# W2 in two pieces a half over four column groups, 128-row adapter fillers, and small loads first: a conditional low-rank block and a recurrence

## The reference

```python
# layer 0, with x: (4, 512, 256), ada_emb = cond: (4, 256)
c = layernorm(ada_emb) * ln_gamma + ln_beta
w = gelu(c @ W1 + bias1) @ W2 + bias2                  # W2: (256, 8192)
a1, b1, a2, b2 = [t.reshape(B, D, R) for t in jnp.split(w, 4, axis=-1)]
u = jnp.einsum('btd,bdr->btr', x, a2)
mid = gelu(jnp.einsum('btd,dl->btl', x, base_down) + jnp.einsum('btr,blr->btl', u, b2))
v = jnp.einsum('blr,btl->btr', b1, mid)
out = jnp.einsum('btl,kl->btk', mid, base_up) + jnp.einsum('bkr,btr->btk', a1, v)
x = x + (x + out)
# layer 1, with h0 = cond
xW = jnp.einsum('ntd,dh->nth', x, Wx) + b
h_t = tanh(xW_t + h_(t-1) @ Wh)                        # 512 steps, one after the other
x = x + hs
```

## Time and profile before

| | us |
|---|---|
| three timed runs | 555.97, 550.74, 555.61 |
| their median | 555.61 |
| the profiled execution | 551.53 |
| its span, first to last instruction | 549.7 |
| TensorE busy | 511.1 (93%) |
| DVE busy | 296.5 (54%) |
| ACT busy | 176.5 (32%) |
| POOL busy | 21.9 (4%) |

### The profile page before, as it was taken

How to read it: one execution, slowest core, us unless ns; L and a number is a source line. 1 busy time by engine, 2 the same in 40 slices (tenths; PEclk the granted TensorE clock), 3 DMA queues, 4 the chain that set the end, 5 groups by cost and what they waited for, 6 DMA issues and landing times.

```text
span 549.7 us, 32433 instructions
## 1 busy us (share of the span) xinstructions
PE 511.1 (93%) x14388; PEld 439.2 (80%) x14388; DVE 296.5 (54%) x2262; ACT 176.5 (32%) x1154; POOL 21.9 (4%) x34
## 2 busy tenths in 40 slices
PE   6988999999999999999998999899999989998995
PEld 4224777899999999999998888888888888888884
DVE  1154666555656555565555555555555555555553
ACT  2010222333333434333333333333333333333322
POOL 2850000000000000000000000000000000000000
PEclk7698999999999999999999999999999999999998
DMA  8950000000000000000000000000000000000000
GB/s 295 383 185 2 3 4 3 13 5 14 4 13 5 14 4 4 16 4 14 4 14 5 14 4 14 4 7 11 5 14 4 13 5 13 4 14 5 8 9 12
DMA packets 11346, 16.01 MB, mean 29 GB/s; under 512 B 1715, under 2 KB 7106, under 8 KB 11202
## 3 DMA queue, kind: packets, MB, share of 16 engines
q1 hardware_dynamic: 10352, 13.37, 7.4%
q10 hardware_dynamic: 854, 0.57, 0.4%
HBM read 11.85 MB, written 2.10 MB: 25 GB/s over the span
## 4 chain that ended last, share of the span: by engine, by line
PE 89%; ACT 5%; issue 2%; DVE 1%; DMA 1%; ACTq 0%; DVEq 0%
PE bank L833 65%; PE bank L762 7%; ACT w_sb L429 5%; PE bank L803 3%; PE bank L808 3%; PE bank L656 2%; PE bank L790 2%; PE bank L649 1%; DMA beta_sb<-in_L_cond_ln_beta 1%; PE bank L771 1%; PE bank L635 1%; PE bank L757 1%; PE bank L671 1%; PE bank L820 1%; PE bank L676 0%
## 5 line engine op out<-in xcount | busy, mean ns | idle before, releaser
L833 PE MATMUL bank<-w_sb,whp 128*128 128x52 bf16 x6132 | 243.0, 186 | 25.1 <-ACT w_sb L429 24.8
L591 DVE TENSOR_TENSOR r_ring<-w_sb 128x4 f32<-128x4 f32 x1022 | 136.5, 163 | 211.6 <-ACT w_sb L429 207.7
L429 ACT ACTIVATE w_sb<-bank 128x4 f32<-128x4 f32 x1024 | 142.0, 173 | 320.8 <-PE bank L833 320.8
L833 PEld LDWEIGHTS bank<-w_sb,whp 128*128 128x128 bf16 x6132 | 188.7, 96 | 68.4 <-ACT w_sb L429 46.4
L833 PE MATMUL bank<-r_ring,whp 128*128 128x52 bf16 x4096 | 219.9, 185 | 0.1
L833 PEld LDWEIGHTS bank<-r_ring,whp 128*128 128x128 bf16 x4096 | 173.9, 96 | 0.2 <-issue 0.2
L833 PE MATMUL bank<-l_ring,whp 128*128 128x52 bf16 (+1 forms) x2048 | 156.4, 177 | 0.0
L596 DVE TENSOR_TENSOR l_ring<-r_ring 128x4 bf16<-128x4 f32 x1024 | 136.3, 162 | 0.0
L833 PEld LDWEIGHTS bank<-l_ring,whp 128*128 128x128 bf16 x2048 | 121.6, 96 | 0.0
L762 PE MATMUL bank<-xp,wxp 128*128 128x32 bf16 x1536 | 71.6, 177 | 0.0
L762 PEld LDWEIGHTS bank<-xp,wxp 128*128 128x128 bf16 x1536 | 54.0, 96 | 0.0
(11 more groups left out here) (109 smaller groups left out, 192.3 us busy)
## 6 DMA issues: line engine op xcount, KB each, us to landing
w_sb<-in_L_cond_W SPq DMA_DIRECT2D x16, 512.0 KB, 10.8
x_sb<-in_x SPq DMA_DIRECT2D x4, 512.0 KB, 11.2
out<-o_sb SPq DMA_DIRECT2D x64, 32.0 KB, 1.6
down_sb<-in_L_cond_base_down SPq DMA_DIRECT2D x1, 256.0 KB, 5.2
w_sb<-in_L_cond_W ACTq DMA_DIRECT2D x1, 256.0 KB, 5.6
up_sb<-in_L_cond_base_up ACTq DMA_DIRECT2D x1, 256.0 KB, 9.0
wx_sb<-in_L_cond_Wx SPq DMA_DIRECT2D x1, 256.0 KB, 10.2
wh_sb<-in_L_cond_Wh SPq DMA_DIRECT2D x1, 256.0 KB, 10.4
```

Of the source, the lines that this page charges most:

```text
L429: nc.scalar.activation(h_ring[:, m, slot(pair, s), 0:B], zt, ACT.Tanh).then_inc(h_ready, 1)
L591: nc.vector.tensor_tensor(r_ring[:, k, q, 0:B], state_before(pair, s, k)[:, 0:B], state_hi_before(pair, s, k)[:, 0:B], ALU.subtract).then_ ...
L833: return nc.tensor.matmul(zbank(p, q, m)[:, col0:col0 + n], whp[part][:, k, P * m:P * (m + 1)], rhs[:, 0:n], start=False, stop=stop, skip_ ...
```

## The change

- **Loads.** W1 goes to SP, ahead of x. ACT issues cond, gamma, beta and bias1 first, and bias2 last, in four DMAs. Each half of W2 comes in four DMAs of 1 MB. ACT loads the table for Gelu right after the square root.
- **W2.** A half has two pieces of two chunks (1024 columns). `w_products` writes all four groups of 32 rows: even and odd chunk of each of the half's two types. There are 4 calls of 8 matmuls. `keep_rank` runs on 128 rows, 4 times. Copies on DVE and ACT bring the odd chunk's rows beside the even one's. The factors have a tile for each half.
- **Adapter products.** `a2m` and `b1m` are 128 rows high, zero outside 32 of them, so each product has 128 rows and is cut in two of 128 columns. ACT makes the masked copies. One list of 64 jobs (`job`), five a tile, two steps each, steps 0 to 9, now orders low-rank and unit products from tile 0, step 4, to tile 13.
- **Rest.** Both halves of v and a1 stand in the prologue. Input products have steps 10 to 15 but for 12: 11, 11, 11, 10 and 9 of them.

```diff
-        fac = sb("fac", [P, D])
+        fac = [sb(f"fac{h}", [P, NPC, 2, DC]) for h in range(2)]
...
-        facm = sb("facm", [P, B, D])
-        b1m = sb("b1m", [Q, B, D])
-        b2s = sb("b2s", [P, D])
+        a2m = sb("a2m", [P, B, D])
+        b1m = sb("b1m", [P, B, D])
...
-        SUMS, TURN, ROWS, PREFETCH = 3, 4, 5, 8
...
-        LOW, UNIT, ROWS_STEP = 1, 3, 12
+        SUMS, TURN, ROWS = 3, 4, 5
+
+
+
+
+
+
+        FILL, NJ, TURN_ROWS = 10, 5, 12
+        FIRST_J = 2
         NUNIT = B * (NTT - 1)
-        REST = {2: 2, 4: 5, 6: 6}
-
-        def unit_of(tile):
-            return 1 + (tile - UNIT) // B, (tile - UNIT) % B
-
-        def is_unit(tile):
-            return UNIT <= tile < UNIT + NUNIT
+        NMAKE = B * 8
+        NFILL = NMAKE + 4 * (NUNIT - B)
+        MOVE = (4, 5, 8, 9, 10)
+        REST = {2: 2, 4: 4, 6: 6}
+        INPUTS = (11, 11, 0, 11, 10, 9)
+        LOW_DOWN, LOW_UP, MID, UP = range(4)
+
+        def job(tile, j):
+            n = NJ * tile + j - FIRST_J
+            if not 0 <= n < NFILL:
+                return None
+            if n < NMAKE:
+                b, w = n // 8, n % 8
+                return (LOW_DOWN, LOW_UP, MID, UP)[w // 2], b, w % 2
+            return (MID, UP)[(n - NMAKE) % 4 // 2], B + (n - NMAKE) // 4, (n - NMAKE) % 2
...
+        def job_out(tile, j):
+            return bank[4 * (1 - tile % 2) + 1 + j % 3][:, P:P + D]
...
-                for c in range(NCH):
+                for c in range(NPC):
                     for k in range(K2):
-                        sp.dma_start(w2_sb[:, k, j:j + 2, CH * c:CH * (c + 1)],
-                                     w2v[k, :, j:j + 2, CH * c:CH * (c + 1)]).then_inc(ld_w2[h][c][k], 16)
-
+                        sp.dma_start(w2_sb[:, k, j:j + 2, 2 * CH * c:2 * CH * (c + 1)],
+                                     w2v[k, :, j:j + 2, 2 * CH * c:2 * CH * (c + 1)]).then_inc(ld_w2[h][c][k], 16)
+
+            sp.dma_start(w1_sb[:], W1.rearrange("(k p) n -> p k n", p=P)).then_inc(ld_w1, 16)
...
+            for h in range(2):
+                nc.gpsimd.memset(fac[h][:], 0.0).then_inc(zeroed, 1)
+            nc.gpsimd.memset(a2m[:], 0.0).then_inc(zeroed, 1)
+            nc.gpsimd.memset(b1m[:], 0.0).then_inc(zeroed, 1)
...
-            act.dma_start(bias2_sb[:], bias2.rearrange("(j n) -> j n", j=NTYPE)).then_inc(ld_bias2, 16)
-            act.dma_start(w1_sb[:], W1.rearrange("(k p) n -> p k n", p=P)).then_inc(ld_w1, 16)
...
+                for t in range(2):
+                    j = min(HALVES[h]) + t
+                    act.dma_start(bias2_sb[NTYPE * h + 2 * t:NTYPE * h + 2 * (t + 1)],
+                                  bias2.rearrange("(j c e n) -> j e c n", j=NTYPE, e=2, n=CH)[j]).then_inc(ld_bias2, 16)
...
+            nc.scalar.preload_act_table(ACT.Gelu)
...
+            act.wait_ge(fac_ready[0], NPC)
+            act.wait_ge(zeroed, 4)
+            nc.scalar.copy(fac[0][ROWS1, :, 1], fac[0][ODD1, :, 0]).then_inc(b2_ready, 1)
...
+            for b in range(B):
+                nc.scalar.mul(a2m[ROWS1, b], factor(0, ROWS0), bmask[ROWS0, b:b + 1]).then_inc(a2m_ready, 1)
...
-                rows = slice(Q * min(HALVES[h]), Q * min(HALVES[h]) + 2 * Q)
                 dve.wait_ge(w_ready[h], c + 1)
-                tmp = wmul[rows, c % 2].rearrange("p (d r) -> p d r", r=RANK)
+                tmp = wmul[:, c].rearrange("p (d r) -> p d r", r=RANK)
                 then_wait(nc.vector.tensor_tensor(
-                    tmp, bank[c][rows, :].rearrange("p (d r) -> p d r", r=RANK),
-                    rmask[rows].unsqueeze(1).broadcast_to([2 * Q, DC, RANK]), ALU.mult))
-                nc.vector.tensor_reduce(fac[rows, DC * c:DC * (c + 1)], tmp, AX.X, ALU.add).then_inc(fac_ready[h], 1)
+                    tmp, bank[NPC * h + c][:].rearrange("p (d r) -> p d r", r=RANK),
+                    rmask[:].unsqueeze(1).broadcast_to([P, DC, RANK]), ALU.mult))
+                nc.vector.tensor_reduce(fac[h][:, c, 0], tmp, AX.X, ALU.add).then_inc(fac_ready[h], 1)
...
+            for c in range(NPC):
                 keep_rank(0, c)
-            keep_rank(1, 0)
+            nc.vector.tensor_copy(fac[0][ROWS0, :, 1], fac[0][ODD0, :, 0]).then_inc(a2_ready, 1)
...
+            def move_low(tile, j, which, b, k):
+                dve.wait_ge(low_psum, 4 * b + 2 * (which - LOW_DOWN) + k + 1)
+                dst, base = (wd, down_sb) if which == LOW_DOWN else (wu, upT)
+                nc.vector.tensor_tensor(dst[:, b, k], job_out(tile, j), base[:, k], ALU.add).then_inc(low_moved, 1)
...
-                    for j in HALVES[h]:
-                        last = nc.tensor.matmul(bank[c][Q * j:Q * (j + 1), :],
+                    for g in range(NTYPE):
+                        j, e = HALVES[h][0] + g // 2, 2 * c + g % 2
+                        last = nc.tensor.matmul(bank[NPC * h + c][Q * g:Q * (g + 1), :],
...
+                    if i < FILL and (made := job(tile, i // 2)):
+                        if made[0] in (LOW_DOWN, LOW_UP):
+                            low_product(tile, i // 2, i % 2, *made)
+                        if made[0] == MID:
+                            mid_product(tile, i // 2, i % 2, made[1], made[2])
+                        if made[0] == UP:
+                            up_product(tile, i // 2, i % 2, made[1], made[2])
+                    if tile < NUNIT and i == TURN_ROWS:
                         turn_rows(tile)
-                    if i >= PREFETCH and not (last and p == 1):
-                        if i == PREFETCH:
+                    if i >= FILL and not (last and p == 1):
+                        if i == FILL:
 
                             pe.wait_ge(xp3_ready, tile + 2)
                             if p == 0 and not first:
                                 pe.wait_ge(o_ready, pair)
                             if tile == 0:
-                                pe.wait_ge(x2_rest, 4)
-                        e = i - PREFETCH
-                        if i < ROWS_STEP or i > ROWS_STEP + 1:
-                            input_products(1 - p, e // 4, e // 2 % 2, [e % 2])
-                        if i == ROWS_STEP + 1:
-                            input_products(1 - p, 1, 0, range(K2))
+                                pe.wait_ge(x2_rest, 6)
+                        e = i - FILL
...
+            def low_product(tile, j, e, which, b, k):
+                if which == LOW_DOWN:
+                    pe.wait_ge(a2m_ready, b + 1)
+                    left, right = a2m, fac[0]
                 else:
                     pe.wait_ge(b1m_ready, b + 1)
-                    left, right = b1m[:, b], fac[Q * A1:Q * (A1 + 1), :]
-                if i >= 3:
-                    pe.wait_ge(low_moved, B * K2 * which + i - 2)
-                nc.tensor.matmul(low_out(LOW + which, i), left[:, P * k:P * (k + 1)], right, start=True,
-                                 stop=True).then_inc(low_psum, 1)
-
-            def unit_product(tile, i):
-                t, b = unit_of(tile)
-                u, n, k = tile - UNIT, i // 2 % K2, i % K2
-                if i == 0:
+                    left, right = b1m, fac[1]
+                ins = nc.tensor.matmul(job_out(tile, j)[:, P * e:P * (e + 1)], left[:, b, P * k:P * (k + 1)],
+                                       right[:, e].rearrange("p e n -> p (e n)"), start=True, stop=True)
+                if e == 1:
+                    ins.then_inc(low_psum, 1)
```

More of the change, by code:

```diff
@@ L517, in make_x2 @@
                     in1=bank[4 + n][:].rearrange("p (b t) -> p b t", b=B)[:, :, t0:t1], op0=ALU.mult, op1=ALU.add)
-            mask_v(0)
+            for h in range(2):
+                mask_v(h)
             for n in range(K2):
@@ L675, in v_product @@
             def v_product(h, k):
-                last = nc.tensor.matmul(columns(bank[6][0:Q, B * HQ * h:B * HQ * (h + 1)]), b1T[:, k],
+                last = nc.tensor.matmul(columns(bank[6 + h][0:Q, 0:B * HQ]), b1T[:, k],
                                         mid0[:, k, :, HQ * h:HQ * (h + 1)], start=(k == 0), stop=(k == K2 - 1))
@@ new lines, in low_product, with mid_product @@
+                    left, right = b1m, fac[1]
[3 more added lines that the diff above has]
+                    ins.then_inc(low_psum, 1)
+            def mid_product(tile, j, k, u, m):
+                t, b = unit_of(u)
+                if k == 0 and m == 0:
+                    pe.wait_ge(rows_moved, u + 1)
+                    if u < B:
+                        pe.wait_ge(low_moved, 4 * b + 2)
+                    else:
+                        pe.wait_ge(x2_fill, K2 * (u - 1))
+                ins = nc.tensor.matmul(job_out(tile, j)[:, 0:P], wd[:, b, k, P * m:P * (m + 1)],
+                                       xT[:, k, b, P * t:P * (t + 1)], start=(k == 0), stop=(k == K2 - 1))
+                if k == K2 - 1:
+                    ins.then_inc(fmid_psum, 1)
@@ new lines, in up_product @@
+            def up_product(tile, j, k, u, n):
+                b = unit_of(u)[1]
```

(8 more changed lines are left out.)

226 lines of the change are left out of this document (101 added, 125 removed).

## The result

The changed kernel takes 547.9 us (median of 20 executions, 537.0 to 550.4), the kernel before 552.7 (median of 20, 550.7 to 557.3). The executions of the changed kernel lie in two groups, 6 at 537.0 to 542.0 and 14 at 546.5 to 550.4. The ratio of times, which compares the lower group with the executions of before, is 0.976, interval 0.973 to 0.980; the two medians alone have the ratio 0.991. The profiled execution took 548.2 us, its span 546.4, and belongs to the upper group.

What follows compares the result with a forecast made beforehand. TensorE was taken as the bound, a prologue to 53.2 us and then 512 steps. From the profiled 551.5 us, -3.3 -1.5 -3.2 -3.5 = -11.5 gave 540.0; for spread between runs it predicted 541.5, range 534 to 549.

Steps and rivals of the forecast that it cites:

- the sum: Whole kernel: prologue -3.3, tile 0 -1.5, tile 1 -3.2, tile 2 -3.5, together -11.5 us from 551.5, so 540.0.
- Fillers: Loop, tiles 1 and 2: products of 128 rows by 128 columns cost nothing, giving back 3.2 and 3.5 us.
- Rival 3: Loop, tiles 0 to 6: low-rank fillers not free, 6.7 us come back, 546.7 us; chance 0.10.
- Tile 0: Loop's first 16 steps: v and a1 products leave, 1.5 us less, bounds 0.7 and 2.2.
- Four column groups: Prologue, W2 products: four groups run side by side, 1.84 us a call, eight calls become four.
- rival 2: Prologue, W2 calls: column groups run in pairs only, 9.1 us more, 549.1 us; chance 0.08.
- factor of 1.3: Prologue, W2 calls: by a speedup of 3.07 a call takes 1.3 times as long, sum 2.7 us higher; not adopted.
- bias2: Prologue: its four DMAs, last on ACT's list, land at 11.0 us and hold all of TensorE's program behind.
- rival 1: Prologue: bias2 lands much later, 17.1 instead of 11, 6.1 us more, 546.1 us; chance 0.12.
- The small loads: Prologue loads: beta's 8.9 us wait goes, but W2 products start at 20.9 instead of 19.8, costing 1.1 us.
- Zeroing on POOL: Prologue: zeroing, ACT's copies and masks cost nothing beside TensorE; an uncovered mask or copy, a few tenths of a us.
- Rival 4: Prologue: granted clock stays at 0.5 past 24.4 up to the loop, slower than before, 562 us; chance 0.04.

Runs made afterwards that it cites:

- both: Changed kernel with the first bias product moved behind the base-down products and POOL's ring memset waiting for DVE's copy of the odd A2 rows; 537.4 us, ratio 0.970.
- bias_product_later: Changed kernel with the first bias product and its wait for the bias2 DMAs moved behind both base-down products; 538.2 us, ratio 0.976.
- memset_after_copy: Changed kernel with POOL's memset of the ring padding waiting until DVE's copy of the odd A2 rows is done; 543.2 us, ratio 0.984.
- changed_five_rounds: Changed kernel, unaltered, in six more executions, the first profiled; 538.6, 537.9, 541.2, 549.1, 541.6 and 549.2 us.
- copy_on_act: Changed kernel with the copy of the odd A2 rows moved from DVE to ACT, POOL's zeroing not made to wait; 540.1 us, ratio 0.976.
- low_rank_256_columns: Changed kernel with each low-rank filler whole, 128 rows by 256 columns, in one step of each pair and none in the other; 553.0 us.

## Why the prediction was right in the loop and wrong in the prologue

The prediction was 541.5 us, 534 to 549. The median, 547.9, lies 6.4 above it, near the upper bound, and the sign and the chance of "faster" were right. That the median is inside the range is luck: the upper part was there for rivals 1 to 3, none of which came, and what filled it was no rival. The lower group, 537 to 542, is the case that the sum describes; 14 of 20 executions are not in it.

**Fillers: right.** Tiles 1 and 2 gave back 3.2 and 3.45 (forecast 3.2 and 3.5). The rule "128 rows by 128 columns costs nothing" from the earlier trace rows carried over to zero-padded rows. Rival 3 falls, and the two experiments on fillers show that its price is real where rows are not filled up or columns not cut.

**Tile 0: right,** 15.45 (forecast 15.8). It still holds one step of 1.34 us whose surplus the chain calls issue; the experiments have 15.05 where that step is missing.

**Four column groups: right.** 16 instructions in 1.85 to 1.90, forecast 1.84; rival 2 falls. The three groups at once of the earlier trace rows were the row to go by. The Trainium skill, "TensorE: Matmul & The Clock Gate", Part 3, gives the speedup of 3.07 for four row tiles; for column tiles, which these are, it has only three (2.38), so the prediction's factor of 1.3 was carried over from another case. This trace has the full four: 16 instructions in four groups take 1.85 to 1.90, and the 4 of the u product, in one group, 1.89 at the high clock.

**bias2: right.** Landed at 10.98, forecast 11.0, so rival 1 (17.1) falls. The order of issue gave 8.9 to 11.7; that 11.0, picked between them, is hit within 0.02 is luck. The prediction also said that it would be late next and hold all of TensorE's program; this costs 3.4 us of W2's start in `both` and 6.9 in bias_product_later. The small loads brought nothing for that reason.

**The step that failed: "Zeroing on POOL, the copies and adapter masks on ACT ... lie beside TensorE's work and are costed at nothing".** The prediction priced DVE's small copy at nothing and POOL's zeroing at nothing, each by itself, and did not ask whether the two meet. What it gave as a bound for an uncovered copy, "a few tenths of a us", was taken from DVE alone and was 4.5. It never laid the new chain's times beside POOL's list, where a single instruction of 5.22 us stood behind the same W2 products. The first step came at 58.1 instead of 49.9, 8.2 later. By the chain: the A2 transposes start at 35.72 instead of 31.1, 4.6 later, of which 4.3 are the hold (a copy of 0.2 would have ended at 31.4). From there to the first step it took 22.35 us instead of 18.8: the u product 1.7 more, the third W2 call 1.1, base-up 0.6, all for the low clock (below). memset_after_copy took the first away and kept the second, and changed_five_rounds shows 18.83 us for that stretch (30.09 to 48.92) when neither happens.

The Trainium skill, "SBUF — State Buffer", "Who interferes with whom", states this: DVE and GpSimd share a pair of ports as an exclusive lock; a DVE copy can run in a mode that takes the pair, whoever issues first then has it for the whole instruction, and ACT never waits. The traces agree: 4.51 us under the zeroing, 1.03 behind a subtraction, 0.30 on ACT; DVE's reduction (L536), which ran under the zeroing from 30.43 on, stayed at 0.69. By that rule and the 5.22 us of L352, a rival of up to 5.2 us could have been worked out beforehand. That ports are the reason no run here shows; the runs show which engines and which instructions hold each other.

**The clock: a term that was left out.** Rival 4 had the clock low all the way, 562 us, and the sum had it high from 24.4 on; in between lay what came, two stretches of 6.8 and 3.4 us at 1.2 GHz for 3.4 us of time. It does not need the hold: in memset_after_copy and copy_on_act stretches of 3.4 us are low with no wait of over 0.94 us, while in changed_five_rounds and `both`, with waits of up to 0.87, the clock stays up. It differs from one execution to the next, and what decides it stays open. With TensorE idle in the hold the low stretch that began there was 6.8 or 17.1 us in all four traces, so part of the low clock of the upper group may still be the hold's. The earlier trace rows showed one execution, and the kernel before has such a stretch too, from 51.7 to 55.1, over its first steps (PEclk 0.94 in the earlier trace rows); that was the sign that a stretch of low clock can come after 24.4.

## What to carry to other kernels

Lay every DVE copy between SBUF tensors on a new critical chain beside POOL's list, by its times: one long POOL instruction can hold a copy of 0.2 us for all its length, whether it does can turn on less than 1 us of drift, and a copy that waits for one POOL instruction can be held by the next one too. A wait on POOL's side, or ACT for the copy, removes it. A step priced at nothing needs the name of what runs beside it on each engine that it could share something with, and not only the engine that hides it.

## What the runs showed of the hardware beyond what was expected

- One program can have two groups of times 8 us apart, for an order between two engines that no semaphore fixes: the copy at 29.77 took 0.22 us, at 30.46 it took 5.2 (zeroing from 30.51 and from 30.34).
- A DVE copy that started 0.41 us ahead of POOL's zeroing, under a cast of POOL, was held through both: 5.71 us (low_rank_256_columns). Wherever it waited for a cast, a subtraction or the zeroing of POOL, it ended 0.07 to 0.08 us behind POOL's instruction.
- The granted clock fell to 1.2 GHz for a few us in the middle of nearly unbroken TensorE work (memset_after_copy at 31.37, waits of 0.21 and 0.39 us before it) in some executions, and not in others of the same work; one such pair of stretches costs about 3.5 us.
- A passage from 128-row to 32-row matmuls and back costs 0.16 us a step here (5.2 us over 32 steps), at the same 0.48 us for the pair of instructions.
